# In the edge MLP, POOL waits at every second quad for the landing of the preceding quad's scatters

## The reference

```python
w_phys = (jax.nn.silu(rbf @ w1 + b1) @ w2 + b2) * cutoff[:, None]     # per edge: 64 -> 256 -> 256
msg_phys = xn[col] * w_phys
...                                                                     # Q, K, V, attention per edge
aggr = jax.ops.segment_sum(msg_phys + gate * msg_attn, row, num_segments=n)
```

## Time and profile before

| | us |
|---|---|
| median of 3 runs | 2454.26 |
| lowest and highest of them | 2453.97, 2462.91 |
| span of the profiled execution | 2759.2 |
| of it, edge MLP (178 to 893) | 715 |
| granted clock of TensorE over the span | 0.912 |

### The profile page before, as it was taken

How to read it: one execution, slowest core, us unless ns; L and a number is a source line. 1 busy time by engine, 2 the same in 40 slices (tenths; PEclk the granted TensorE clock), 3 DMA queues, 4 the chain that set the end, 5 groups by cost and what they waited for, 6 DMA issues and landing times.

```text
span 2759.2 us, 46196 instructions
## 1 busy us (share of the span) xinstructions
PE 2167.8 (79%) x10682; PEld 1608.5 (58%) x10683; DVE 1809.3 (66%) x4269; ACT 1490.9 (54%) x5784; POOL 1440.6 (52%) x1468
## 2 busy tenths in 40 slices
PE   0688787778785798888888988828888788888884
PEld 0356566666664676767676766615556565555552
DVE  8962222222222699999898989736776777676776
ACT  2234444444443677777777776525555555554550
POOL 5345555566556655555565653254555555455540
PEclk9999899998988899999999999968998999898996
DMA  6332222222222889899999986032222222222231
GB/s 205 121 141 105 92 102 94 99 99 104 102 88 87 302 302 308 295 309 298 302 303 302 304 295 210 32 82 57 77 76 71 78 73 79 73 76 72 74 63 47
DMA packets 153333, 413.85 MB, mean 150 GB/s; under 512 B 40848, under 2 KB 53045, under 8 KB 153282
## 3 DMA queue, kind: packets, MB, share of 16 engines
q0 software_dynamic: 79360, 301.93, 34.1%
q1 hardware_dynamic: 73922, 111.33, 12.5%
HBM read 328.69 MB, written 84.60 MB: 150 GB/s over the span
## 4 chain that ended last, share of the span: by engine, by line
PE 30%; DVE 28%; issue 17%; another core or an unknown queue 12%; DMA 4%; DVEq 3%; ACT 3%; POOL 1%; SPq 1%; ACTq 0%; POOLq 0%
PE ps L1316 12%; DVE gmx L1177 5%; PE ps L1465 4%; DVE arena L1015 3%; DVE sc L1029 3%; PE ps L1302 2%; DVE arena L1206 2%; DMA arena<-sorted_edges 2%; PE ps L1349 2%; DVE work L1038 2%; PE ps L1364 2%; DVE arena L1022 2%; PE ps L1352 2%; DVEq L313 1%
## 5 line engine op out<-in xcount | busy, mean ns | idle before, releaser
L574 POOL DMA_INDIRECT arena<-node_row,idxC x464 | 452.8, 976 | 418.4 <-DVE arena L1206 271.7
L511 POOL DMA_INDIRECT sorted_edges<-work,idxA x416 | 410.3, 986 | 298.0 <-issue 297.7
L1316 PE MATMUL ps<-w_sb,arena 128*128 128x256 f32 x1664 | 432.6, 417 | 129.1 <-DVE work L986 129.0
L986 DVE TENSOR_TENSOR work<-ps,b_bc 128x512 f32<-128x512 f32 x208 | 141.9, 690 | 499.8 <-PE ps L1316 242.7
L1316 PEld LDWEIGHTS ps<-w_sb,arena 128*128 128x128 f32 x1664 | 337.4, 209 | 219.1 <-DVE work L986 126.0
L1465 PE MATMUL ps<-arena,hq 128*128 128x260 f32 x928 | 289.6, 440 | 108.0 <-DVE work L1172 76.8
L643 ACT ACTIVATE work<-work 128x256 f32<-128x256 f32 x416 | 184.7, 499 | 261.1 <-DVE work L986 231.3
L531 POOL DMA_INDIRECT work<-node_kvx,idxB x232 | 236.1, 1018 | 169.3 <-issue 61.9
L531 POOL DMA_INDIRECT arena<-node_kvx,idxB x232 | 232.3, 1001 | 175.8 <-issue 67.4
L1177 DVE TENSOR_REDUCE gmx<-ps 128x4 f32<-128x1024 f32 x232 | 282.5, 1218 | 48.8 <-remote 28.4
L1349 PE MATMUL ps<-arena,work 128*128 128x256 f32 x928 | 254.1, 397 | 61.3 <-issue 52.1
(11 more groups left out here) (187 smaller groups left out, 4482.7 us busy)
## 6 DMA issues: line engine op xcount, KB each, us to landing
arena<-sorted_edges SPq DMA_DIRECT2D x232, 260.0 KB
arena<-in_edge_attr SPq DMA_DIRECT2D x25, 512.0 KB
node_kvx<-arena SPq DMA_DIRECT2D x24, 384.0 KB, 2.3
arena<-node_row,idxC POOLq DMA_INDIRECT x464
sorted_edges<-work,idxA POOLq DMA_INDIRECT x416
sorted_edges<-arena SPq DMA_DIRECT2D x25, 260.0 KB, 2.1
sorted_edges<-arena SPq DMA_DIRECT2D x1, 6240.0 KB, 20.2
arena<-node_kvx,idxB POOLq DMA_INDIRECT x232
```

Of the source, the lines that this page charges most:

```text
L511: pool.indirect_dma_start(rec_dram[:, :], bass.IndirectOffsetOnAxis(ap=idxA[:, st.slot(8), c:c + 1], axis=0), recA[:, st.slot(8), c, :], N ...
L574: pool.indirect_dma_start(row1_g[:, st.slot(16), j, :], None, row1_dram[:, :], bass.IndirectOffsetOnAxis(ap=idxC[:, batch(st).slot(4), st. ...
L1316: ins = pe.matmul(ps[:, 5 + t, half * H:(half + 1) * H], hidT[:, r, m, half, t * P:(t + 1) * P], w2_sb[:, m, :], start=m == 0, stop=m == 1)
```

## The change

Ahead of a quad's four scatters, and only at every second quad (even step numbers, quad 0 left out), POOL waits until the four scatters of the quad before have landed. Nothing else is touched: no DMA, buffer or engine is added or moved.

```diff
@@ -506,6 +506,9 @@
                     return
                 pool.wait_ge(s("idxA_ready"), st.n + 1)
                 pool.wait_ge(s("rows_cut"), st.n + 1)
+                if st.u % 2 == 0 and not st.first(1):
+                    before = st.back(1)
+                    pool.wait_ge(s(f"scattered{before.slot(8)}"), 64 * before.turn(8) + 64)
                 alone(pool)
                 for c in range(4):
                     pool.indirect_dma_start(
```

## The result

| | before | after |
|---|---|---|
| median, us | 2454.11 (4 runs) | 2576.61 (4 runs) |
| lowest and highest, us | 2452.99, 2462.91 | 2571.12, 2584.99 |
| ratio to before | | 1.0482, 95% interval 1.0459 to 1.0506 |
| span of the recording, us | 2759.2 | 2569.2 |

The changed kernel is slower by 4.8%, 122 us by the medians and 113 to 124 by the interval. I had forecast 2550, 2495 to 2572: the sign and the mechanism hold, the size was 27 us too small and the time lies outside the range. Most striking is the last row of the table. By their recordings the changed kernel is 190 us *faster*, by their runs it is 122 slower; none of the four timed runs of the kernel before took more than 2462.91 us.

A forecast was written before the change was run, and what follows sets the result against it. POOL was taken to bound the edge MLP in timed runs free of stalls. Its 531 us plus 101 for 51 waits less 5 of cover gave 627, so +96 us on 2454: 2550 us, range 2495 to 2572.

The forecast's parts named there:

- The bound: Edge MLP, timed runs: POOL back to back at 5.11 us a quad sets the stage's end, PE needing 4.93.
- The first lead: Profiled execution: its 305 us over the median nearly equal the chain's 331 us for "another core or an unknown queue".
- the long add: DVE's 6.82 us add L998, beside which one scatter took 6.43 us; claimed to be no part of the difference.
- The third rival: POOL's scatters quicker in timed runs, 1.20 us: 2536 us, or 2497 with cheap waits; chance 0.18 together with cheap waits.
- The price of one wait: POOL's scatters, edge MLP: landing 2.39 plus start 0.87 less step 1.28, 1.98 us each, 101 us for 51 waits.
- The cover: Edge MLP: what starved POOL before is absorbed after, hiding up to some 10 us of 101; 5 taken off.
- The range: Whole kernel: 2495 us for cheap waits with faster POOL, to 2572 for 112 us of waits; 0.2 chance beyond.
- The profiled span: Changed kernel's profiled execution: POOL's 632 us still fit into the stage's 715, so span within some 15 us of 2759.
- the stalls: "Remote" waits in MLP (219 us) and layer 1 (104 us), taken as cost of recording PE's instructions, absent from timed runs.
- The first (the stalls are in the timed runs, POOL has slack): Edge MLP: POOL's idle time takes the waits up, perhaps 6 us left, 2460 us; chance 0.11.
- the second (scatters in a row cause them): Edge MLP: waits break POOL's rows of scatters, so stalls go, 64 us less, 2390 us; chance 0.05.
- The fourth (the wait is met anyway): POOL's added waits: a target already met costs nothing; held only if POOL comes late anyway; no chance of its own.

The follow-up runs named there:

- clean recording: Kernel before, unchanged, recorded a second time, with no wait for "remote"; 2459.92 us, ratio 0.9987, span of the recording 2456.0 us.

## Why the prediction was right or wrong

**The bound: right.** I took POOL for the engine that sets the pace in the timed runs, against the recording at hand, in which it was idle for 297.7 us of the stage and the chain showed it with 0.8%. The first lead was that the gap between span and median and the chain's unexplained share were one size. The clean recording gives 536.5 us from first to last scatter where I had 531 without the long add. The third rival, a POOL that is quicker in a timed run, falls with the clean recording too: its steps are the same 1.28 us, in a span of 2456.

**The price of one wait: mis-sized.** This is the step that failed, with the two below. The sum had 2.39 + 0.87 - 1.28 = 1.98 us and 101 us in all. Measured are 2.17 us on average and 110.5 in all. Most of the surplus stands in every wait: 46 of the 51 cost 2.03 to 2.14 us. The landing in the middle of the run took 2.42 to 2.50, mostly 2.45, where the trace tells it (26 of the 51), not the 2.39 of the very last scatter; the start after it took 0.87 us in most of these, as I had it, and 0.96 or more in others. The rest are a few landings that come late, as 3.95 us of idle time ahead of quad 4:

```profile
220.47 0.97 POOL L514 DMA_INDIRECT sorted_edges<-work,idxA  x1 [3.95 <-DMA sorted_edges<-work,idxA]
```

**A term that the sum lacked, 5.7 us.** At quads 28, 50, 72 and 94, every 88 scatters, the second scatter behind a wait comes 1.42 us late:

```profile
370.18 0.97 POOL L514 DMA_INDIRECT sorted_edges<-work,idxA  x1 [2.44 <-ACT idxA L628]
372.89 0.98 POOL L514 DMA_INDIRECT sorted_edges<-work,idxA  x1 [1.74 <-issue]
```

The kernel with every quad waiting has it at the same four quads, the one with every fourth at 28 and 72, where it waits, and not at 50 and 94; among the scatters of the clean recording of before it is at none. POOL's register moves ahead of the scatters, which the trace holds as well, show why. Two of them are 2.71 us apart where two in a row are otherwise 0.54: 369.96 and 372.67 here, at the scatters given above. The clean recording of before has the same pair, at 332.52 and 335.23, only that POOL's instruction list is three scatters further ahead of the work there, and the scatters go on at 1.28. The same four pairs of moves, 88 scatters apart, are so far apart in all recordings but the one with the wait behind the second scatter, which has gaps of 2.67 us at two places. So POOL's instruction list stops for a moment at fixed places, which a list that is ahead of its engine hides and one that has just waited does not. With the wait behind the first scatter it falls behind the release itself and costs more, 2.93 instead of 0.76 us. A wait for a landing is not needed for it: with PE slower and no waits added, POOL stands idle before each quad, and the second scatter of quad 28 begins 2.71 us after the first there too. What the stop is stays open.

**The cover: wrong by 5 us.** I took 5 us off because POOL might have been starved before here and there; in the clean recording it was not, once.

Added up: 110.5 + 5.7 - 1.9 (the long add holds a scatter for 5.12 us now and for 7.01 before) = 114.3, and the stage grew by 650.6 - 536.5 = 114.1 us. That is 18 over my 96. The two recordings differ by 2569.2 - 2456.0 = 113.2. The 122 by the medians are 8 us more. Nothing shows where these lie: the interval begins at 113, the rest of the span is the same in both recordings (1918.6 and 1919.4), and over all eleven it varies by up to 19 us. So 18 of the 27 us by which the forecast missed are accounted for, and the rest may be the spread of the runs, which is not shown.

**The range: too short above.** I had closed it at 2572 with 112 us as the dearest case for the waits, an end built on one undisturbed landing and a guess of half a microsecond for disturbance. The waits came to 110.5, so that end held for them alone; what put the time outside are the 5.7 us of the stops and the 8 that stay open (2454 and 114 would have been 2568, inside). Its lower end was 55 us from the forecast and its upper end 22, although nearly every landing that the trace tells was later than that row. A range for a wait should reach up further than down.

**The profiled span: wrong.** I expected the stalls in every recording of this kernel, and therefore a span within 15 us of 2759. It was 2569.2. The step behind this one that failed is "the cost of recording PE's many instructions": it was a feature of one recording. What held is only its consequence, that the stalls are not in the timed runs. (The news of the matmuls in the earlier trace rows was also 7.1 us late by its lines, 613.13 to 620.22, not some 8; nothing in the sum hangs on it.) That the gap would shrink to about 210 if the step was right is refuted the same way; it shrank to 7.

**The rivals.** The first (the stalls are in the timed runs, POOL has slack) and the second (scatters in a row cause them) fall with the clean recording; the slower PE shows what the first would have looked like. The fourth (the wait is met anyway) is true with the target one quad further back, at a cost of nothing, and with two scatters in between.

## What to carry to other kernels

A wait for one's own DMA costs what landing and start-up take less what the engine still has to do in that time, and all of it lands on the end only if that engine sets the pace: here mostly 2.1 us with nothing in between, 0.8 behind one scatter, nothing behind two, and nothing ahead of the quad when PE was slower by 1.5 us a quad than POOL. Before costing a change, set the span of the recording beside the median of the runs; where they differ by a tenth, ask which rows belong to the recording, and work out each engine's pace from a stretch without holes.

## What the runs showed of the hardware that I had not expected

A program on one core can be recorded with holes of up to 10.3 us in which an engine waits although the matmuls that it needs can be shown as finished (for 7.1 us in the earlier trace rows), 305 us over the median in all, while eleven other recordings of it and of its variants had none. And POOL's instruction list has a stop of 2.7 us every 88 scatters, in the kernel before as well, which costs 1.42 us where POOL has just waited, 2.2 where it falls right behind the release, and nothing where the list is ahead of the engine.
